# A two-block window-attention network on one core: the second block's scores made in one batch per group, and the first GELU placed ahead of a copy

## The reference, cut to what matters

```python
xn = layernorm(x, g1, b1)
windows, Hp, Wp = window_partition(xn, WS)              # WS = 8: 49 windows of 64 tokens per image
attn = jnp.einsum('bnhd,bmhd->bhnm', q, k)              # q scaled by 1/sqrt(16)
attn = jax.nn.softmax(attn, axis=-1)
out = jnp.einsum('bhnm,bmhd->bnhd', attn, v)
x = shortcut + (out @ w_proj + b_proj)
h = layernorm(x, g2, b2)
h = jax.nn.gelu(h @ w_fc1 + b_fc1, approximate=False)   # 96 -> 384
return x + (h @ w_fc2 + b_fc2)                          # 384 -> 96
```

## Time and profile before

| what | value |
|---|---|
| median of three runs | 7380.75 us (7376.72 to 7386.88) |
| the profiled execution | 7375.31 us, of which its span is 7373.5 us |
| PE busy in the span | 7154.4 us, 97% |
| ACT, DVE, POOL busy | 6372.4, 6160.1, 5239.8 us |
| granted TensorE clock, mean | 0.992 |
| first block ends, second has its first bodies | about 4430 and 4460 us |

### The profile page before, as it was taken

One profiled execution on the slowest core, in us unless ns is written; L12 is line 12 of the kernel. 1 busy time (PEld: TensorE's weight loads), 2 busy tenths in 40 slices (PEclk: granted clock), 3 DMA queues, 4 the chain that ended last, 5 costly groups with the idle time before them and its releaser, 6 DMA issues. The chain is left out here.

```text
span 7373.5 us, 316562 instructions
## 1 busy us (share of the span) xinstructions
PE 7154.4 (97%) x113246; PEld 5501.1 (75%) x113246; DVE 6160.1 (84%) x12718; ACT 6372.4 (86%) x11836; POOL 5239.8 (71%) x5957
## 2 busy tenths in 40 slices
PE   6999999999999999999999996999999999999999
PEld 4777777777777777777777775777777777777777
DVE  5888888888888888888888875887887887887886
ACT  5999999999999999999999986877787787887887
POOL 3777777777777777777777775666666666666665
PEclk9999999999999999999999998999999999999999
DMA  0111111111111111111111101111111111111111
GB/s 22 30 29 30 30 29 31 29 30 30 30 30 29 30 30 30 29 30 30 30 30 30 29 23 26 29 30 28 30 29 29 30 29 30 29 30 29 30 30 26
DMA packets 342619, 214.35 MB, mean 29 GB/s; under 512 B 265624, under 2 KB 341144, under 8 KB 341144
## 3 DMA queue, kind: packets, MB, share of 16 engines
q1 hardware_dynamic: 341146, 194.49, 10.7%
HBM read 78.66 MB, written 77.07 MB: 21 GB/s over the span
## 5 line engine op out<-in xcount | busy, mean ns | idle before, releaser
L881 POOL TENSOR_TENSOR swin_score<-swin_score,swin_top 113x588 f32<-113x588 f32 x1024 | 1202.9, 1175 | 738.9 <-DVE swin_top L753 738.4
L624 ACT ACTIVATE swin_probT<-swin_ps_probs 128x339 f32<-128x339 f32 x2048 | 921.9, 450 | 197.5 <-PE swin_ps_probs L481 176.2
L1558 POOL TENSOR_TENSOR plain_k_heads<-plain_k_hat,plain_head_mask 96x512 f32<-96x512 f32 x392 | 398.9, 1037 | 916.5 <-ACT plain_k_hat L1356 916.5
L481 PE MATMUL swin_ps_probs<-swin_ident,swin_prob 113*128 113x113 f32 x6144 | 990.6, 270 | 7.0 <-ACT swin_probT L624 7.0
L481 PEld LDWEIGHTS swin_ps_probs<-swin_ident,swin_prob 113*128 113x128 f32 x6144 | 667.5, 141 | 355.1 <-issue 321.4
L748 DVE TENSOR_TENSOR swin_score<-swin_ps_scores,swin_bias_tab 113x588 f32<-113x588 f32 x1024 | 777.8, 760 | 173.7 <-PE swin_ps_scores L471 172.8
L753 DVE TENSOR_REDUCE swin_top<-swin_score 113x12 f32<-113x588 f32 x1024 | 768.9, 751 | 0.2
L630 ACT ACTIVATE swin_prob<-swin_score 113x588 f32<-113x588 f32 x1024 | 719.0, 702 | 5.4 <-POOL swin_score L881 2.5
L784 DVE SCALAR_TENSOR_TENSOR swin_x<-swin_y,swin_y_rstd,swin_x_res 98x96 f32<-98x96 f32 x1024 | 601.7, 645 | 0.8 <-POOL swin_y_rstd L899 0.7
L1436 DVE TENSOR_REDUCE plain_top<-plain_ps_scores 128x6 f32<-128x384 f32 x784 | 432.4, 552 | 190.2 <-PE plain_ps_scores L1206 171.5
L495 PEld LDWEIGHTS swin_ps_mixed<-swin_probT,swin_v_heads 128*32 128x32 f32 x24576 | 422.3, 109 | 223.3 <-issue 146.8
(11 more groups left out here) (188 smaller groups left out, 21082.6 us busy)
## 6 DMA issues: line engine op xcount, KB each, us to landing
swin_k_heads<-swin_k_hat SPq DMA_DIRECT2D x1024, 36.8 KB
plain_x_in<-between_blocks SPq DMA_DIRECT2D x784, 48.0 KB, 2.2
out_dram<-plain_x SPq DMA_DIRECT2D x784, 48.0 KB, 2.0
swin_x_in<-in_x SPq DMA_DIRECT2D x224, 136.5 KB
between_blocks<-swin_x SPq DMA_DIRECT2D x224, 136.5 KB
swin_x_in<-in_x SPq DMA_DIRECT2D x224, 19.5 KB
between_blocks<-swin_x SPq DMA_DIRECT2D x224, 19.5 KB
swin_x_in<-in_x SPq DMA_DIRECT2D x224, 2.6 KB
```

Of the source, the lines that this page charges most:

```text
L481: last = nc.tensor.transpose(psP[:, n * QT:(n + 1) * QT], prob[0:QT, p, 2 * hp:2 * hp + 2, :].rearrange('p h k -> p (h k)'), ident[0:QT, 0 ...
L624: nc.scalar.activation(to, psP[:, 0:3 * QT], ACT.Copy).then_inc(did['probT'], 1)
L881: nc.gpsimd.tensor_tensor(view, view, bcast(top[0:QT, p % 2, :], 2, WIN), ALU.subtract).then_inc(did['shifted'], 1)
```

## The change: what it does

In the second block `scores` loses its argument h. One call at the top of the body makes all 24 matmuls of the group's four pairs, each pair in columns of its own, so that the three banks are filled whole. It waits for `shifted` of the last pair of the group before, and it raises `scored` once per group. `scores(0, 1)` in the middle of the body is gone, so `mix(-1, 1)` follows `hidden(-3, 2, B)` at once. `shift` reads each pair at its own columns and waits for the one count; `bias_q` and `spread_keys` count alike. On ACT, `gelu(-3, 0, B)` stands ahead of `copy_turned(-1, 3)`. The first block is the same.

```diff
--- before.py
+++ after.py
@@ -1192,18 +1192,17 @@
                                 pe.wait_ge(did[name], upto(g + d, *place))
                                 break
 
-                    def scores(d, h):
+                    def scores(d):
                         if exists(g + d, groups):
                             pe.wait_ge(did['q_hat'], upto(g + d))
-                            pe.wait_ge(did['k_heads'], upto(g + d, h, 2))
-                            ug, uh = earlier_half(g + d, h)
-                            pe.wait_ge(did['shifted'], upto(ug, 2 * uh + 1, PAIRS))
-                            for p in (2 * h, 2 * h + 1):
+                            pe.wait_ge(did['k_heads'], upto(g + d, 1, 2))
+                            pe.wait_ge(did['shifted'], upto(g + d - 1, PAIRS - 1, PAIRS))
+                            for p in range(PAIRS):
                                 for half in range(2):
                                     w = 2 * p + half
                                     for band in range(BANDS):
                                         part = slice(32 * band, 32 * band + 32)
-                                        last = nc.tensor.matmul(psS[half * HALF:half * HALF + WIN, band, p % 2 * BC:(p % 2 + 1) * BC], q_hat[part, parity(d), w * WIN:(w + 1) * WIN], k_heads[part, parity(d), :, w * WIN:(w + 1) * WIN], start=True, stop=True)
+                                        last = nc.tensor.matmul(psS[half * HALF:half * HALF + WIN, band, p * BC:(p + 1) * BC], q_hat[part, parity(d), w * WIN:(w + 1) * WIN], k_heads[part, parity(d), :, w * WIN:(w + 1) * WIN], start=True, stop=True)
                             last.then_inc(did['scored'], 1)
 
                     def mix(d, h):
@@ -1289,7 +1288,7 @@
                                 last = nc.tensor.transpose(psT[0:DIM, p * TT:(p + 1) * TT], x1_norm[:, p, :], ident[0:TT, 0:TT])
                             last.then_inc(did['x1_turned'], 1)
 
-                    scores(0, 0)
+                    scores(0)
                     mix(-1, 0)
                     free(('v_heads', 0), ('hid', -4, 1, CHUNKS), ('x1', -3), ('k_hat', 0))
                     keys(1, A)
@@ -1305,7 +1304,6 @@
                     hidden(-3, 1, A)
                     free(('hid', -3, 0, CHUNKS), ('q_hat', 1), ('x2', -4))
                     hidden(-3, 2, B)
-                    scores(0, 1)
                     mix(-1, 1)
                     free(('hid', -3, 1, CHUNKS), ('x1', -2), ('k_hat', 1), ('v_heads', 0))
                     values(1, A)
@@ -1395,8 +1393,8 @@
                     copy_turned(-1, 2)
                     exponentials(0, 1)
                     act.preload_act_table_set(GELU_SET)
+                    gelu(-3, 0, B)
                     copy_turned(-1, 3)
-                    gelu(-3, 0, B)
                     gelu(-3, 1, A)
                     gelu(-3, 2, B)
                     act.preload_act_table_set(EXP_SET)
@@ -1429,10 +1427,10 @@
                     def shift(d, p):
                         if exists(g + d, groups):
                             dve.wait_ge(did['prob'], upto(g + d - 1, p, PAIRS))
-                            dve.wait_ge(did['scored'], upto(g + d, p // 2, 2))
+                            dve.wait_ge(did['scored'], upto(g + d))
                             shifted = score[0:QT, p, :].rearrange('p (b j k) -> p b j k', j=J, k=WIN)
                             greatest = top[0:QT, p, :].rearrange('p (b j) -> p b j', j=J)
-                            from_psum = psS[0:QT, :, p % 2 * BC:(p % 2 + 1) * BC].rearrange('p b (j k) -> p b j k', k=WIN)
+                            from_psum = psS[0:QT, :, p * BC:(p + 1) * BC].rearrange('p b (j k) -> p b j k', k=WIN)
                             nc.vector.tensor_reduce(greatest, from_psum, AX.X, ALU.max).then_inc(did['top'], 1)
                             dve.wait_ge(did['top'], upto(g + d, p, PAIRS))
                             nc.vector.tensor_tensor(shifted, from_psum, bcast(greatest, 3, WIN), ALU.subtract).then_inc(did['shifted'], 1)
@@ -1445,7 +1443,7 @@
                     def bias_q(d, bank):
                         if exists(g + d, groups):
                             dve.wait_ge(did['q_made'], upto(g + d))
-                            dve.wait_ge(did['scored'], upto(g + d - 2, 1, 2))
+                            dve.wait_ge(did['scored'], upto(g + d - 2))
                             nc.vector.tensor_scalar(q_hat[:, parity(d), :], psM[0:DIM, bank, 0:NT], b_qk[:, 0:1], None, ALU.add).then_inc(did['q_hat'], 1)
 
                     def residual(d, bank):
@@ -1553,7 +1551,7 @@
                     def spread_keys(d, h):
                         if exists(g + d, groups):
                             pool.wait_ge(did['k_hat'], upto(g + d))
-                            pool.wait_ge(did['scored'], upto(g + d - 2, 1, 2))
+                            pool.wait_ge(did['scored'], upto(g + d - 2))
                             tokens = slice(2 * h * TT, 2 * (h + 1) * TT)
                             nc.gpsimd.tensor_tensor(k_heads[0:DIM, parity(d), :, tokens], bcast(k_hat[:, tokens], 1, J), bcast(head_mask[:, :], 2, 2 * TT), ALU.mult).then_inc(did['k_heads'], 1)
```

## The result

The changed kernel takes 7419.93 us (median of five, 7416.66 to 7421.44) against 7380.75 us (7376.72 to 7386.88): 1.0052 times the kernel before, with a 95% interval of 1.004 to 1.0064. It is slower, as forecast, but by 39 us and not by 97; the stated range began at 7440 us. The profiled execution has a span of 7418.1 us, 44.6 us more than before.

What follows compares the result with a forecast made beforehand. The ACT loop (14.55 us) was taken to bind, the DVE loop 0.08 us behind; scores moved make the latter 11.66 + 3.27 + 0.15 = 15.08 us, +0.53 over 192 bodies: 102 us, forecast 7478 us, range 7439 to 7500.

Steps and rivals of the forecast that it cites:

- ACT loop: Third hidden chunk, PE through keys, ACT's bias_k to first GELU, next third chunk; 14.55 us, setting the period before.
- DVE loop: mix(-1, 1) through project, DVE's residual to normalise(-1, 0), next mix; 14.47 us before, forecast 15.08 after the change.
- handover: From the end of DVE's normalise to the start of the mix on PE: 0.15 us, possibly 0.04.
- GELU ahead of the copy, 0.23 us off the ACT loop: On ACT, the first GELU starts at 6015.73 instead of 6015.96, making the ACT loop 14.32 us.
- The copy holds nobody: ACT's copy of pair 3, now behind the first GELU, is done by 6017.41 and delays no reader.
- `mixedT` becomes the wait: On PE, mix(-1, 1) waits for DVE in every body, about 190 times, some 0.5 to 0.75 us each.
- Score matmuls moved, +0.61 us on the DVE loop: The 12 middle score matmuls, moved to the top, lengthen PE's part from 11.05 to 11.66 us.
- lower bound of 0.52: Least cost in us of the 12 score matmuls moved to the top, if a 0.09 us turn is saved.
- 25 ns each: Pace claimed for score records on PE within one stream, from 0.61 us over 24 records.
- The bounds: Per body, +0.33 us with handover and score streams cheapest, +0.62 us dearest; range 7439 to 7500 us.
- DVE's list isn't the longer way: On DVE, shift(0, 0) starts 0.61 us later, but residual waits for project, which is just as much later.
- The rival of nearly free extra scores: At the top, 24 more score records cost about 0.1 us, so time stays 7380 us; chance 0.04.

Runs made afterwards that it cites:

- gelu_only: The kernel before with only the first GELU put ahead of ACT's copy of pair 3: 7362.41 us, 0.998 times the kernel before.
- dve_only: The kernel before with only DVE reordered, normalise(-1, 0) ahead of partial_x1(-2) and moments_x1(-2) behind shift(0, 2): 7382.96 us, 1.0 times the kernel before.
- gelu_dve: The kernel before with the first GELU ahead of the copy and the DVE order of dve_only: 7336.6 us, 0.9947 times the kernel before.
- two_streams: The changed kernel with the top's 24 score matmuls split in two streams, mix(-1, 0) between them: 7623.37 us, 1.0323 times the kernel before.
- scores_dve: The changed kernel without its GELU part and with the DVE order of dve_only: 7342.99 us, 0.9944 times the kernel before.
- after_dve: The changed kernel with the DVE order of dve_only: 7306.27 us, 0.9906 times the kernel before.
- after_dve_turn: after_dve with the four transposes turn_x(2) moved on PE to just ahead of mix(-1, 1): 7325.1 us, 0.9923 times the kernel before.

## Why the prediction was right or wrong

- **What bounds the kernel before** was right: two loops within 0.1 us of each other, the ACT loop ahead. gelu_only reaches 14.48 us, where the prediction had 14.47 for the DVE loop, and dve_only shows that it didn't bind. The match to 0.01 us is partly luck: the handover in it was taken from bodies near the end of the program with no scores ahead of the mix, and gelu_only has nearly the same 0.14 us with scores ahead of it.
- **GELU ahead of the copy, 0.23 us off the ACT loop**: right; gelu_dve's 14.33 us against the 14.32 forecast. The copy holds nobody, as said. In the changed kernel the third hidden chunk is 0.24 us late (6014.12, where 6013.65 + 0.23 was possible), as expected.
- **The DVE loop takes over, and `mixedT` becomes the wait**: right in its place, its releaser and its count (every one of the 161 bodies in the stretch). The stretch on DVE was 3.27 us, as forecast.
- **Score matmuls moved, +0.61 us on the DVE loop: this term failed.** It was 0.35: PE's part grew from 11.05 to 11.40 us. I took the price of a whole stream of 24 records, 0.61 us, for 24 more records in a stream that is already there. Their own price is 24 x 18 ns = 0.43 us; the fixed 0.17 us is paid once for the merged stream. Even the lower bound of 0.52 kept too much of it: it allowed for the 0.09 us between the two streams, not for the gap that both have. So the added records cost 0.18 us less than assumed. Another 0.09 us was saved in the stream that was already there, which took 0.70 and not 0.61 before. There, the mix at the top starts at 6010.74, 0.10 us after the end of ACT's copy of pair 1 (6010.15 + 0.49); in the changed kernel that copy ends at 6007.94, long before the mix at 6008.39. gelu_only, gelu_dve and two_streams have the same 0.10 us from the end of that copy to the mix. That this wait explains the 0.09 us is read from the timelines, not tested by itself. And the "25 ns each" was a misreading: 0.61 / 24 has the fixed gap in it, while the weight loads of the same stream, 0.44 us for 24, gave 18 ns.
- **The handover of 0.15 us: the second wrong term.** It was 0.05 in the changed kernel. The 0.15 us came from one instance near the end of the program, and there the changed kernel shows it again (7392.37 to 7392.52). I had 0.04 as the other end and chose the instance on the same wait. The two errors, 0.26 and 0.10 us, are all of the difference between the forecast +0.53 and the measured +0.17 us per body.
- **For the ACT loop the move of the scores was put at nothing: this failed too**, without any effect on the forecast, since that loop doesn't bind in the changed kernel. One stream takes 1.05 us in place of 0.70 and 0.61, and scores_dve is 0.21 us per body below the kernel before.
- **The bounds** failed with the first term: +0.33 us was the least they allowed. The lower end, 7439 us, also lacks the 5.4 us from the profiled execution to the median, which the forecast and the upper end have; with it, it would be 7444.
- **DVE's list isn't the longer way**: right, with the 0.21 us of idle time still there; two_streams shows how little room that is.
- **The rival of nearly free extra scores** was wrong in size too, though it asked the right question: the extra records were cheaper than the average of a stream, 18 ns and not 25, but far from the 0.1 us for 24 that it needed.

## What to carry to other kernels

When a piece of work is merged into a stream that is already there, price it by the slope between streams of different length, not by the cost of a whole stream; where the trace has only one length, look how the stream's time divides between its weight loads and the gap behind them, and let the lower bound be one without the gap. In a pipeline with several engines, write down each closed loop with its length before judging a move. What a move does to the time depends on which loops it enters or leaves, and a loop 0.1 us behind caps the gain from shortening the first. Two edits can be worth nothing or a loss alone and 1% together: scores and GELU without DVE's new order cost 39 us; with it they save about 70, since dve_only stands at 1.0 times the kernel before and after_dve at 0.9906.

## What the runs showed of the hardware that was not expected

- A merged score stream costs 18 ns per record (1.05 us for 48, 1.92 us for 96) and about 0.17 us once, in front of the next step's weights.
- The same handover, from the end of DVE's `normalise` to the mix on PE, takes 0.05 us in the bodies of the changed kernel and of after_dve, and 0.14 us in those of gelu_only, where a score stream stands in front of the mix; near the end of the program it is 0.15 us, with PE idle as it is in the changed kernel's bodies. What makes the difference stays open.
- An operation on DVE and one on POOL lengthen each other, and which of them pays depends on which starts first. `xT_low` on DVE takes 0.69 us, and `x_res` on POOL (line 1540, or 1542 in the kernels built on the one before) 1.00 us, where they don't overlap, as in the changed kernel. In after_dve_turn POOL starts first, by 0.05 us:

```profile
6003.88 1.50 DVE L1508 TENSOR_TENSOR plain_xT_low<-plain_xT,plain_xT_high 96x512 fp32r<-96x512 f32 x1 [0.67 <-ACT plain_xT_high L1387]
```

```profile
6003.83 1.00 POOL L1540 TENSOR_TENSOR plain_x_res<-plain_x_in,plain_res_row 128x384 f32<-128x384 f32 x1
6004.79 0.65 POOL L1546 TENSOR_TENSOR plain_var_eps<-plain_moments,plain_epsilon 128x4 f32<-128x4 f32 x1
```

In gelu_dve DVE starts first, by 0.04 us, and it is POOL that takes longer:

```profile
6010.57 0.69 DVE L1510 TENSOR_TENSOR plain_xT_low<-plain_xT,plain_xT_high 96x512 fp32r<-96x512 f32 x1 [0.59 <-ACT plain_xT_high L1389]
```

```profile
6010.61 1.51 POOL L1542 TENSOR_TENSOR plain_x_res<-plain_x_in,plain_res_row 128x384 f32<-128x384 f32 x1
```

after_dve is like the first (mean of `xT_low` 1466 ns over 168 bodies, 695 ns over 162 of the changed kernel), dve_only like the second (`x_res` 1.52 us). In after_dve, after_dve_turn and scores_dve `xT_low` ends 0.54 to 0.55 us after `x_res`, though it starts from 0.04 to 0.32 us behind it. That the later one stands until the other is done is the reading of these timelines; no run was made to test it. It costs nothing on the DVE loop here: in after_dve_turn `shift(0, 0)`, behind `xT_low`, still has to wait for PE (0.61 us idle).
